# Queries projected in the second half of layer one instead of being kept in DRAM, and the residual added in layer two

## The reference

```python
xn = _layernorm(x)
x = x + gnn(xn, ..., src, dst) + mix(xn[None], Wq, Wkv, Wproj, bproj)[0]
x = x + ffn(_layernorm(x)[None], ...)[0]

# gnn: twice, with 8 heads of 64 and then 1 head of 256
e = leaky_relu(el[src] + er[dst], 0.2)
alpha = softmax of e over the edges of one dst
out = segment_sum(alpha[:, :, None] * feat[src], dst)

# mix: linear attention, 8 heads of 32
q, k = elu(xn @ Wq.T) + 1, elu(xn @ Wk.T) + 1
context, k_sum = einsum('bhnd,bhne->bhde', k, v), k.sum(2)
mix = (q @ context) / max(q @ k_sum, 1e-6) @ Wproj.T + bproj
```

## Time and profile before

| | us |
|---|---|
| median of 3 runs | 3636.33 (3636.3 to 3638.42) |
| the profiled execution | 3636.28 |
| its span | 3634.4 |
| layer one, first row gather issued to last | 420.4 to 1774.4 |

### The profile page before, as it was taken

One profiled execution on the slowest core, in us unless ns is written; L12 is line 12 of the kernel. 1 busy time (PEld: TensorE's weight loads), 2 busy tenths in 40 slices (PEclk: granted clock), 3 DMA queues, 4 the chain that ended last, 5 costly groups with the idle time before them and its releaser, 6 DMA issues. The chain is left out here.

```text
span 3634.4 us, 37755 instructions
## 1 busy us (share of the span) xinstructions
PE 2213.0 (61%) x8126; PEld 1372.6 (38%) x8126; DVE 2594.4 (71%) x6161; ACT 1905.4 (52%) x6135; POOL 2350.2 (65%) x2057
## 2 busy tenths in 40 slices
PE   5960044444444444544545540079999999999999
PEld 3540022232223223332323320045555555555565
DVE  8987378888888888888865643366666666666742
ACT  1210067777776667666733333256565655555642
POOL 0004788888888888888646547777777777777500
PEclk9985566666665555555567875589999999999999
DMA  6321389999999999999944435766666666666510
GB/s 189 94 74 21 115 316 348 341 342 346 343 347 338 356 371 363 362 358 369 341 156 115 114 79 170 226 196 201 199 202 200 204 201 203 199 199 199 183 44 11
DMA packets 279436, 821.07 MB, mean 226 GB/s; under 512 B 71711, under 2 KB 149135, under 8 KB 257694
## 3 DMA queue, kind: packets, MB, share of 16 engines
q0 software_dynamic: 126496, 377.09, 34.5%
q1 hardware_dynamic: 121790, 420.89, 30.4%
q10 hardware_dynamic: 30944, 20.94, 2.1%
HBM read 425.16 MB, written 394.56 MB: 226 GB/s over the span
## 5 line engine op out<-in xcount | busy, mean ns | idle before, releaser
L1323 POOL DMA_INDIRECT e_rows<-scratch_table,k_src x1680 | 1975.0, 1176 | 514.1 <-issue 345.8
L1435 ACT ACTIVATE e_rows<-e_rows,e_wr 128x64 f32<-128x64 f32 (+1 forms) x4200 | 1202.1, 367 | 3.6
L1415 DVE SCALAR_TENSOR_TENSOR e_ring<-e_ring,e_kext,e_rows 128x512 f32<-128x512 f32 (+1 forms) x1568 | 964.2, 615 | 226.1 <-ACT e_rows L1435 135.9
L2071 PE MATMUL e_p_y<-e_wfo,e_h 128*112 128x256 f32 x1792 | 418.7, 388 | 40.8 <-DVE e_y L1833 40.7
L2057 PE MATMUL e_p_b<-e_h,e_wf 128*128 128x448 f32 x896 | 374.8, 563 | 19.5 <-ACT e_h L1980 19.5
L2071 PEld LDWEIGHTS e_p_y<-e_wfo,e_h 128*112 128x112 f32 x1792 | 321.9, 181 | 152.0 <-ACT e_h L1980 60.7
L2045 PE MATMUL e_p_a<-e_xt,e_wf 128*128 128x448 f32 x896 | 358.7, 544 | 0.7 <-ACT e_xt L1995 0.7
L1980 ACT ACTIVATE e_h<-e_p_a,e_shift,e_scale 128x448 f32<-128x448 f32 x224 | 160.3, 721 | 281.6 <-PE e_p_a L2045 281.6
L978 PE MATMUL e_p_c<-e_vext,e_kphi 112*128 112x129 f32 x224 | 68.1, 458 | 374.5 <-DVE e_kphi L868 374.5
L1833 DVE SCALAR_TENSOR_TENSOR e_y<-e_p_y,e_w,e_y 112x256 f32<-112x256 f32 x448 | 194.3, 475 | 96.5 <-PE e_p_y L2071 96.4
L1383 DVE TENSOR_TENSOR e_rows<-e_rows,e_wr 128x3840 f32<-128x3840 f32 x56 | 232.6, 4153 | 13.5 <-ACT e_wr L1428 13.5
(11 more groups left out here) (393 smaller groups left out, 3763.3 us busy)
## 6 DMA issues: line engine op xcount, KB each, us to landing
scratch_sums<-e_ring SPq DMA_DIRECT2D x56, 2112.0 KB, 9.7
scratch_sums<-e_ring SPq DMA_DIRECT2D x56, 1848.0 KB, 9.4
scratch_sums<-e_ring SPq DMA_DIRECT2D x56, 1032.0 KB, 4.5
scratch_sums<-e_ring SPq DMA_DIRECT2D x56, 903.0 KB
e_rows<-scratch_table,k_src POOLq DMA_INDIRECT x1680, 4.8
scratch_table<-na_frow ACTq DMA_DIRECT2D x56, 227.5 KB, 2.3
scratch_table<-hi_frow ACTq DMA_DIRECT2D x56, 115.5 KB, 2.1
na_x<-in_x SPq DMA_DIRECT2D x7, 896.0 KB, 17.3
```

What stands on the lines that cost most here:

```text
L1323: nc.gpsimd.indirect_dma_start(out=rows[:, n % B, g, :], out_offset=None, in_=table, in_offset=bass.IndirectOffsetOnAxis(ap=k.src[:, n * G ...
L1415: nc.vector.scalar_tensor_tensor(ring[:, i, j - c0, 0:W], prev, kext[:, 0, j + 1:j + 2], rows[:, rb, j, 0:W], ALU.mult, ALU.add).then_inc( ...
L1435: last = nc.scalar.activation(rows[:, rb, j, at], rows[:, rb, j, at], ACT.Copy, scale=wr[:, b, h, j + 1:j + 2])
L2071: last = nc.tensor.matmul(self.p_y[bank][0:BK, i * D:(i + 1) * D], self.h2[:, e % 2, kt, v:v + BK], self.wfo[:, e, kt, :], start=kt == 0, ...
```

## The change

In the first half, `project` makes only keys and values; the queries are neither computed nor stored. In the second half the turned tiles are read a second time, `query` (TensorE) projects them, `query_exponents` (ScalarE) and `query_features` (VectorE) make elu + 1 into `q` in SBUF. `residual` goes: ScalarE copies the output from PSUM (`result`), and `x` is read in layer two, 448 KB a round, and added there by one VectorE instruction (`add_input`). `turn_back` gets a PSUM tile of its own.

```diff
     def sync(self, sp, n, half):
         t = self.tiles(n)[half]
         if n < self.HALF:
-            sp.wait_ge(self.q_kept, t + 1)
-            sp.dma_start(self.k.queries[:, t * 2 * BK:(t + 1) * 2 * BK], self.qt[:, :]).then_inc(self.q_out, 16)
-            if t + 2 < NB:
-                self.load_turned(sp, t + 2)
-            else:
-                sp.wait_ge(self.q_out, 16 * (t + 1))
-                self.load_query(sp, half)
-        else:
+            sp.wait_ge(self.projected, t + 1)
+            self.load_turned(sp, t + 2)
+        else:
+            if t + 2 < NB:
+                self.load_turned(sp, NB + t + 2)
             sp.wait_ge(self.res_ready, t + 1)
             sp.dma_start(self.a["res"][t * BK:(t + 1) * BK, :], self.res[:, t % 2, :]).then_inc(self.res_out[t % 2], 16)
-            if t + 2 < NB:
-                self.load_query(sp, t + 2)
...
+    def query_features(self, dve, t):
+        dve.wait_ge(self.q_exp_ready, t + 1)
+        wait(dve, self.ad_ready, t - 1)
+        self.nc.vector.scalar_tensor_tensor(self.q[:, t % 2, :], self.p_q[:, 0:2 * BK], 0.0, self.exps[:, D:D + 2 * BK],
+                                            ALU.max, ALU.add).then_inc(self.q_kept, 1)
...
-    def residual(self, dve, t):
-        nc = self.nc
-        dve.wait_ge(self.o_ready, t + 1)
-        dve.wait_ge(self.x_in[t % 2], t // 2 * 16 + 16)
-        wait(dve, self.res_out[t % 2], t // 2 * 16)
-        nc.vector.tensor_tensor(self.res[:, t % 2, :], self.p_c[0:BK, 0:D], self.x[:, t % 2, :],
-                                ALU.add).then_inc(self.res_ready, 1)
...
             if n == self.HALF and j == 1:
                 self.spread(dve)
-            if j == 2:
+            if n == self.HALF and j == 2:
+                self.query_features(dve, t0)
+            if j == 3:
                 self.quotient(dve, t0)
             if j == 6:
-                self.residual(dve, t0)
-            if j == 8:
+                self.query_features(dve, t1)
+            if j == 9:
                 self.quotient(dve, t1)
-            if j == 12:
-                self.residual(dve, t1)
+            if j == 12 and n < NB - 1:
+                self.query_features(dve, t0 + 2)
...
+    def query_exponents(self, act, t):
+        nc = self.nc
+        act.wait_ge(self.q_projected, t + 1)
         wait(act, self.q_kept, t)
+        nc.scalar.activation(self.low[:, D:D + 2 * BK], self.p_q[:, 0:2 * BK], ACT.Relu, scale=-1.0).then_inc(self.q_low_ready, 1)
+        act.wait_ge(self.q_low_ready, t + 1)
         nc.scalar.activation(self.exps[:, D:D + 2 * BK], self.low[:, D:D + 2 * BK], ACT.Exp, scale=-1.0
+                             ).then_inc(self.q_exp_ready, 1)
...
+    def result(self, act, t):
+        act.wait_ge(self.o_ready, t + 1)
+        wait(act, self.res_out[t % 2], t // 2 * 16)
+        self.nc.scalar.copy(self.res[:, t % 2, :], self.p_c[0:BK, 0:D]).then_inc(self.res_ready, 1)
...
             if j == 4:
+                self.query_exponents(act, t1)
+            if j == 5:
                 self.turn(act, t0)
-            if j == 10:
+            if j == 7:
+                self.result(act, t0)
+            if j == 10 and n < NB - 1:
+                self.query_exponents(act, t0 + 2)
+            if j == 11:
                 self.turn(act, t1)
+            if j == 13:
+                self.result(act, t1)
...
+    def query(self, pe, t):
+        nc = self.nc
+        pe.wait_ge(self.xt_in[t % 2], (NB + t) // 2 * 16 + 16)
         wait(pe, self.q_kept, t)
-        for kt in range(2):
-            nc.tensor.matmul(self.p_kv[0:BK, :], self.xt[:, t % 2, kt, :], self.wkv[:, kt, :], start=kt == 0, stop=kt == 1)
         for m in range(2):
             for kt in range(2):
                 last = nc.tensor.matmul(self.p_q[:, m * BK:(m + 1) * BK], self.wq[:, kt, m * P:(m + 1) * P],
                                         self.xt[:, t % 2, kt, :], start=kt == 0, stop=kt == 1)
-        last.then_inc(self.projected, 1)
+        last.then_inc(self.q_projected, 1)
...
+        wait(sp, self.x_added, g)
+        sp.dma_start(self.x[:, :, :], self.a["x"][bass.ds(row, GN), :].rearrange("(n p) d -> p n d", p=BK)
+                     ).then_inc(self.x_in, 16)
+
+    def add_input(self, dve, g):
+        dve.wait_ge(self.res_in[g % 3], 16 * (g // 3 + 1))
+        dve.wait_ge(self.x_in, 16 * (g + 1))
+        y = self.y[:, g % 3, :, :]
+        self.nc.vector.tensor_tensor(y, self.x[:, :, :], y, ALU.add).then_inc(self.x_added, 1)
...
         if kq == 2:
             if j == 3:
                 self.below(dve, g)
+            if j == 5:
+                self.add_input(dve, g)
```

More of the change, by code:

```diff
@@ L796, in __init__ @@
         self.p_kv, self.p_q, self.p_c = s.ps("p_kv", [P, 512]), s.ps("p_q", [P, 512]), s.ps("p_c", [P, 512])
+        self.p_t = s.ps("p_t", [P, 512])
         self.loaded, self.zeroed, self.step = s.sem("qkv_loaded"), s.sem("zeroed"), s.sem("ctx_step")
@@ L818, in sync_first, with load_turned @@
             self.load_turned(sp, t)
-    def load_turned(self, sp, t):
-        wait(sp, self.projected, t - 1)
+    def load_turned(self, sp, u):
+        if u < NB + 2:
+            wait(sp, self.projected, u - 1)
+        else:
+            sp.wait_ge(self.q_projected, u - NB - 1)
+        t = u % NB
         sp.dma_start(self.xt[:, t % 2, :, :].rearrange("p m v -> p (m v)"),
                      self.k.turned[:, t * 2 * BK:(t + 1) * 2 * BK]).then_inc(self.xt_in[t % 2], 16)
[L825 to L829, removed]
     def sync(self, sp, n, half):
@@ L941, in turn @@
         wait(act, self.o_ready, t)
-        self.nc.scalar.copy(self.att_t[:, :], self.p_q[:, 0:2 * BK]).then_inc(self.att_kept, 1)
+        self.nc.scalar.copy(self.att_t[:, :], self.p_t[:, 0:2 * BK]).then_inc(self.att_kept, 1)
+    def result(self, act, t):
+        act.wait_ge(self.o_ready, t + 1)
+        wait(act, self.res_out[t % 2], t // 2 * 16)
+        self.nc.scalar.copy(self.res[:, t % 2, :], self.p_c[0:BK, 0:D]).then_inc(self.res_ready, 1)
     def scalar(self, act, n, j):
@@ L951, in scalar @@
         else:
+            if n == self.HALF and j == 1:
+                self.query_exponents(act, t0)
             if j == 4:
+                self.query_exponents(act, t1)
+            if j == 5:
                 self.turn(act, t0)
-            if j == 10:
+            if j == 7:
[3 more added lines that the diff above has]
+            if j == 11:
                 self.turn(act, t1)
+            if j == 13:
+                self.result(act, t1)
     def project(self, pe, t):
@@ L964, in project @@
         pe.wait_ge(self.xt_in[t % 2], t // 2 * 16 + 16)
+        wait(pe, self.phi_ready, t)
+        for kt in range(2):
+            last = nc.tensor.matmul(self.p_kv[0:BK, :], self.xt[:, t % 2, kt, :], self.wkv[:, kt, :], start=kt == 0, stop=kt == 1)
+        last.then_inc(self.projected, 1)
+    def query(self, pe, t):
+        nc = self.nc
+        pe.wait_ge(self.xt_in[t % 2], (NB + t) // 2 * 16 + 16)
         wait(pe, self.q_kept, t)
-        for kt in range(2):
-            nc.tensor.matmul(self.p_kv[0:BK, :], self.xt[:, t % 2, kt, :], self.wkv[:, kt, :], start=kt == 0, stop=kt == 1)
         for m in range(2):
@@ L988, in weigh @@
             pe.wait_ge(self.ctx_spread, 1)
-            pe.wait_ge(self.q_kept, NB)
-        pe.wait_ge(self.q_in[t % 2], t // 2 * 16 + 16)
+        pe.wait_ge(self.q_kept, t + 1)
         for m in range(2):
@@ L1000, in turn_back @@
         for m in range(2):
-            last = nc.tensor.transpose(self.p_q[:, m * BK:(m + 1) * BK], self.att[:, m * P:(m + 1) * P], k.ident[0:BK, 0:BK])
+            last = nc.tensor.transpose(self.p_t[:, m * BK:(m + 1) * BK], self.att[:, m * P:(m + 1) * P], k.ident[0:BK, 0:BK])
         last.then_inc(self.turned, 1)
@@ L1031, in tensor @@
             else:
+                if n == self.HALF:
+                    self.query(pe, t0)
                 self.weigh(pe, t0)
+                self.query(pe, t1)
                 if q is not None:
@@ L1041, in tensor @@
                 self.weigh(pe, t1)
+                if n < NB - 1:
+                    self.query(pe, t0 + 2)
                 if q is not None:
@@ L1674, in __init__ @@
         self.y = s.sb("y", [BK, 3, KB, D])
+        self.x = s.sb("x", [BK, KB, D])
+        self.x_in, self.x_added = s.sem("x_in"), s.sem("x_added")
         self.stats = s.sb("stats", [BK, KB, 6])
@@ L1878, in join @@
         if i == 0:
-            dve.wait_ge(self.res_in[g % 3], 16 * (g // 3 + 1))
+            dve.wait_ge(self.x_added, g + 1)
         c.done()
@@ L2161, in gps_kernel @@
         k.turned = scratch("turned", (P, NB * 2 * BK))
-        k.queries = scratch("queries", (P, NB * 2 * BK))
         k.dst_pad = scratch("dst_pad", ((Q + 2) * CAP,), I32)
```

21 lines of the change are left out of this document (8 added, 13 removed).

## The result

The changed kernel takes 3661.18 us (median of 4 runs, 3658.55 to 3661.46) against 3637.38 for the kernel before on the same chip (3636.3 to 3641.03): a ratio of 1.0062, 95% interval 1.0045 to 1.0079. It is slower by 24 us; 3656 was forecast. The profiled execution took 3661.17, against 3636.28.

What follows compares the result with a forecast made beforehand. POOL's gather queue was taken as the bound, level with VectorE in layer one's second half. The terms 0 + 13 + 6 + 1 = +20 us on the span's 3634.4, with 1.9 around it, gave 3656; range 3618 to 3676.

Steps and rivals of the forecast that it cites:

- First half 0: Layer one's first half: removed query work lies beside POOL's queue, so cost 0, with 7 us allowed either way.
- the cover: Layer one's first half: POOL's 25.0 us a group of gathers, beside which the removed work was said to lie.
- Second half +13: Layer one's second half: slower by 13 us, chosen between POOL's pace (0 to +21) and the closed loop (+22).
- the loop: Second half: L1383, quotient, turn, TensorE's output, ScalarE's copy and rows, next group's exponential; 23.7 us a group, closed.
- The upper bound: Second half: the closed loop makes four groups 100.0 us against 96.8, +22 us over 27 groups.
- Layer two +6: Layer two: `add_input` holds up a POOL gather in 13 rounds, +6 us, from 0 to +14.
- at most 1.1 us, some 0.45 on average: Layer two: how long one `add_input` of 1.2 us holds up a gather; at least nothing between two points.
- Last chain +1: End of layer two: `add_input` lies in the chain from the last gather's landing through VectorE to TensorE, +1.2 us.
- The DMA bound: Rival, layer one: full DMA engines are the bound, removed moves save some 36 us, 3607; faster case, chance 0.2.
- VectorE's relief: Rival, second half: losing the 29.3 us wait saves 1.2 us a group, 32 us, 3611; faster case, chance 0.2.
- Hidden: Rival: clock rises, POOL keeps 24.2 us in the second half, `add_input` falls between gathers' points; 0 + 0 + 1, 3637; chance 0.2.
- An instruction with a PSUM operand is harmless: Gathers: only VectorE instructions with two SBUF operands hold them up; one with a PSUM operand assumed not to.

Runs made afterwards that it cites:

- e8: Kernel before, with the second operand of VectorE's 3840-element multiplication in layer one in PSUM: ratio 0.9869 to the kernel before, second chip.
- e4: Changed kernel without TensorE's matmul of the projection bias (output lacks the bias): ratio 0.9983 to the kernel before, first chip.
- e9: Changed kernel with TensorE's bias matmul issued ahead of its wait for the turned tile: ratio 1.0144 to the kernel before, third chip.
- e3: Changed kernel with ScalarE's output copies behind rows 9 and 14 instead of 7 and 13: ratio 1.0049 to the kernel before, first chip.
- e1: Changed kernel with layer two's addition cut to one column of each 256, load of x kept: ratio 1.0032 to the kernel before, first chip.
- e6: Kernel before with x taken out of `residual` (plain VectorE copy), loaded and added in layer two: ratio 1.001 to the kernel before, second chip.
- e5: Changed kernel with neither load nor addition of x in layer two (output lacks x): ratio 1.019 to the kernel before, second chip.

## Why the prediction was right, point by point

- **First half 0.** Right, -1.6. With POOL as the bound, work taken off four other resources bought nothing; VectorE's wait at the logits rose from 50.0 to 68.8 us in 600, as forecast. e8 shows the cover's size from the other side: take POOL's hold-ups away and 43 us come at once.
- **Second half +13.** The size was right (+15.4) and so was the mechanism: e4 and e9 show the loop quotient, turn, output, result, rows. It was drawn too small. I saw the copy's wait as its hinge; e3 removed that wait and, as ScalarE's wait for the queries (60.3 us) and the order of TensorE's queue let me read it, the loop closed again by the query matmuls; no run tested that reading. The upper bound rested on one round before (96.8 us for four groups), quicker than the mean: 660.5 / 27 x 4 = 97.9. After, 675.9 / 27 x 4 = 100.1, as forecast (100.0). The difference to the mean is 2.2 and not 3.2 for four groups, and 27 / 4 x 2.2 = 15. That 13 comes so near is in part luck: it was a choice between 0 and 22, not a sum. The clock, which might have shortened the loop, rose from 0.51 to 0.55 only (the earlier trace rows and the window of after), and the loop took its whole length; what an output takes at 2.4 GHz, put at 1.6 us less, no run shows.
- **Layer two +6.** Too small, +12.5, but inside its bounds of 0 to 14. `add_input` took 1.22 us, as worked out. The failed step is "at most 1.1 us, some 0.45 on average": the ring's operation right behind it prolongs the hold-up, to a longest gather of 2.31, and no average applies, since the addition met a gather in all of the 12 rounds in which row gathers still run beside it, for 12.4 us in all, 1.03 each. The load of x costs nothing that the trace shows: the other gathers and POOL's idle time are as before. e1 gives only 5.5 us back by its profile, since other gathers were held up longer in it; why they were is open. The two rows are of 2530:3430, before and e1; after has 1049.

```profile
L1323 POOL DMA_INDIRECT e_rows<-scratch_table,k_src x593 | 610.9, 1030 | 180.7 <-issue 133.1 <-DVE e_ring L1415 44.5 <-DVE e_ring L1396 2.7
```

```profile
L1343 POOL DMA_INDIRECT e_rows<-scratch_table,k_src x593 | 617.5, 1041 | 180.8 <-issue 131.1 <-DVE e_ring L1435 45.7 <-DVE e_ring L1416 4.0
```

- **Last chain +1.** Not seen (-0.7).
- **The rivals.** The DMA bound fell with e6. VectorE's relief didn't come: its 29.3 us wait in front of `residual` went, but the ring's wait for rows rose from 6.2 to 55.6 us in 600. "Hidden" needed the shorter loop; e4 has one and is level with the kernel before in time, though by a second half 7.8 us under and a layer two 13.7 us over it.
- **An instruction with a PSUM operand is harmless**: an assumption then, shown by e8 for the multiplication. The Trainium skill (SBUF — State Buffer, "Who interferes with whom") says that a VectorE instruction with two SBUF inputs contends with a GpSimd instruction that reads SBUF; e8 agrees, with gathers of 0.95 us where one input is in PSUM. Its inference that a `tensor_tensor` spares descriptor generation doesn't help these gathers, which took 4.40 us in the earlier trace rows and 2.14 beside L1772. They read their row numbers (`k_src`) from SBUF, and no run tells whether that reading or the making of descriptors is what is held up.

## What to carry to other kernels

Find the engine that never stops, and then what makes each of its instructions longer: here a multiplication on another engine, where one operand in PSUM gave 1.3% of the time (e8). Moving a copy to an idle engine isn't free when that engine then waits in order for a third one, ahead of work that the bound needs; draw the whole loop and shorten what is in it, by issuing ahead of the wait what doesn't need it. Take the pace of a stage from all its groups, not from one round, and don't average over meetings that the kernel's own rhythm repeats: `add_input` met a gather in 12 rounds of 12.

## What the runs showed of the hardware beyond that

On the second and third chip every kernel's layer two was longer (1418.7 to 1436.3 against 1232.1 to 1245.8 on the first), and the change without its input's part cost 76 us in the second half (741.4 in e5 against 665.3 in e6) instead of 15. The timeline of e5_no_input on the second chip, at a place like the one shown above:

```profile
1594.05 1.19 PE L1026 MATMUL e_p_c<-e_bproj,e_one 1*112 1x256 f32 x2
...
1598.13 0.37 ACT L942 COPY e_res<-e_p_c 112x256 f32<-112x256 f32 x1 [4.20 <-issue]
...
1599.55 0.75 DVE L1435 SCALAR_TENSOR_TENSOR e_ring<-e_ring,e_kext,e_rows 128x512 f32<-128x512 f32 x1 [4.02 <-ACT e_rows L1455]
```

TensorE's matmul ends at 1595.24 (a modelled end) and ScalarE, idle and with nothing else in front, starts its copy 2.89 us later; on the first chip it was 0.03 (1640.67 to 1640.70). In e5's second half 27 of ScalarE's 105 waits for TensorE end over 0.5 us after the matmul, 52.0 us in all; in e6, on the same chip, it is 1 of 61, and in after, on the first chip, none of 102. ScalarE's waits that the trace puts down to "remote" or "issue" in 1200:1800 are of this kind; in e5:

```profile
ACT e_low L929 <- remote: 22.2, 8, 4.1
ACT e_res L942 <- remote: 17.0, 4, 5.7
ACT e_att_t L937 <- remote: 13.2, 10, 3.9
```

In 25 of the 27 the trace has the update of TensorE's semaphore just before ScalarE's start: what comes late is the update, and ScalarE follows it at once. What delays the update I can't tell from the trace, and no run tested it. But a change that adds hand-overs from TensorE to ScalarE to a closed loop was 0.6% slower on one chip and, even without its input's part, 1.9% on another, while the first half took the same time on all three (678.2 to 681.2 with the multiplication as it was).
